# Attention and eight routed experts on one core: the gate weights of a block brought to the working buffer by two DMA transfers

## The reference

```python
def _expert_ffn(xf, Wi_e, bi_e, Wg_e, bg_e, Wo_e, bo_e, g_e, b_e):
    h = jax.nn.gelu(xf @ Wi_e + bi_e, approximate=False) * jax.nn.sigmoid(xf @ Wg_e + bg_e)
    r = xf + (h @ Wo_e + bo_e)
    mu = jnp.mean(r, axis=-1, keepdims=True)
    var = jnp.mean(jnp.square(r - mu), axis=-1, keepdims=True)
    return (r - mu) * jax.lax.rsqrt(var + EPS) * g_e + b_e
...
probs = jax.nn.softmax(xf @ Wr + br, axis=-1)
topw, topi = jax.lax.top_k(probs, K)      # K = 2 of E = 8
topw = topw / jnp.sum(topw, axis=-1, keepdims=True)
...
out = jnp.einsum('te,eth->th', c, y)      # c holds topw at topi, zero elsewhere
```

## Time and profile before

| | before |
|---|---|
| median of 3 runs | 1213.47 us |
| profiled execution, span | 1213.3 us |
| PE busy | 1083.0 us (89%) |
| VectorE (DVE) busy | 984.6 us (81%) |
| ScalarE (ACT) busy | 803.3 us (66%) |
| GpSimd (POOL) busy | 764.5 us (63%) |
| expert stage, first up matmul | 803.26 us |

### The profile page before, as it was taken

How to read it: one execution, slowest core, us unless ns; L and a number is a source line. 1 busy time by engine, 2 the same in 40 slices (tenths; PEclk the granted TensorE clock), 3 DMA queues, 4 the chain that set the end, 5 groups by cost and what they waited for, 6 DMA issues and landing times. The chain is left out here.

```text
span 1213.3 us, 27322 instructions
## 1 busy us (share of the span) xinstructions
PE 1083.0 (89%) x8520; PEld 819.8 (68%) x8520; DVE 984.6 (81%) x2792; ACT 803.3 (66%) x1804; POOL 764.5 (63%) x1359
## 2 busy tenths in 40 slices
PE   3898999999999999999999998159999999999920
PEld 1565666666666666666666664159999999999920
DVE  4776778888888888878888874659999999999959
ACT  1565666666676676666666666458888888888810
POOL 2257476676676576576576576726777777777740
PEclk9999999999999999999999999569999999999965
DMA  5223446334434434434434421521111121111138
GB/s 146 95 84 112 142 138 198 120 100 137 135 98 126 137 99 135 135 93 132 143 99 116 137 62 34 157 74 50 54 55 54 55 59 56 54 54 57 33 131 305
DMA packets 138270, 127.36 MB, mean 105 GB/s; under 512 B 71848, under 2 KB 96432, under 8 KB 138128
## 3 DMA queue, kind: packets, MB, share of 16 engines
q1 hardware_dynamic: 127184, 103.59, 28.9%
q0 software_dynamic: 8640, 17.84, 4.5%
q10 hardware_dynamic: 2304, 4.20, 0.9%
HBM read 71.13 MB, written 54.43 MB: 103 GB/s over the span
## 5 line engine op out<-in xcount | busy, mean ns | idle before, releaser
L821 ACT ACTIVATE probs<-st 128x384 f32<-128x384 f32 (+1 forms) x768 | 390.7, 526 | 177.2 <-PE st L709 165.3
L867 DVE TENSOR_REDUCE neg_max<-sa 128x2 fp32r<-128x1024 f32 (+3 forms) x384 | 392.9, 1034 | 121.4 <-PE sa L694 120.7
L647 POOL TENSOR_SCALAR_AFFINE_SELECT probs<-probs 128x128 f32<-128x128 f32 (+1 forms) x768 | 246.5, 333 | 228.7 <-ACT probs L821 220.5
L709 PE MATMUL st<-q_stack,k_pad 128*128 128x256 f32 (+2 forms) x1024 | 336.4, 370 | 9.1 <-ACT probs L821 6.6
L689 PE MATMUL sa<-k_pad,q_stack 128*128 128x256 f32 (+2 forms) x1024 | 325.4, 361 | 17.6 <-DMA k_pad<-k_scratch 10.7
L689 PEld LDWEIGHTS sa<-k_pad,q_stack 128*128 128x128 f32 x1024 | 177.5, 190 | 108.9 <-issue 72.7
L1023 POOL DMA_INDIRECT y_scratch<-z,to_row x142 | 190.0, 1338 | 35.9 <-issue 35.9
L709 PEld LDWEIGHTS st<-q_stack,k_pad 128*128 128x128 f32 x1024 | 175.6, 190 | 45.3 <-ACT probs L821 29.0
L1057 PE MATMUL up<-xt_hi,w_cur 128*128 128x256 f32 x568 | 167.3, 294 | 0.0
L722 PE MATMUL pv<-probs,v_aug 128*32 128x512 f32 (+3 forms) x2048 | 166.0, 442 | 0.0
L1058 PE MATMUL up<-xt_lo,w_cur 128*128 128x256 f32 x568 | 161.6, 285 | 0.0
(11 more groups left out here) (161 smaller groups left out, 1435.6 us busy)
## 6 DMA issues: line engine op xcount, KB each, us to landing
q_stack<-q_scratch SPq DMA_DIRECT2D x64, 256.0 KB, 2.7
k_pad<-k_scratch SPq DMA_DIRECT2D x256, 64.0 KB, 2.4
xg<-rows_scratch SPq DMA_DIRECT2D x71, 130.0 KB, 2.1
q_scratch<-q_hi SPq DMA_DIRECT2D x16, 512.0 KB, 3.1
k_scratch<-k_hi SPq DMA_DIRECT2D x16, 512.0 KB, 2.9
y<-y_scratch SPq DMA_DIRECT2D x16, 512.0 KB, 5.6
q_scratch<-q_lo SPq DMA_DIRECT2D x17, 256.0 KB, 3.2
k_scratch<-k_lo SPq DMA_DIRECT2D x17, 256.0 KB, 3.1
```

The costliest lines, as they stand in the source:

```text
L647: pool.affine_select(out=blk, in_=blk, compare_op=ALU.is_ge, fill=0.0, base=0, pattern=[[0, w], [1, P]], channel_multiplier=-1).then_inc(m ...
L709: last = nc.tensor.matmul(st[:, t % 2, at:at + w], k_pad[:, G * g + j, kk * P:(kk + 1) * P], q_stack[:, g, S - w:S], start=True, stop=True)
L821: nc.scalar.activation(probs[:, n % 2, j, lo:lo + w], st[:, k % 2, at:at + w], ACT.Exp).then_inc(exp_done, 1)
L867: V.tensor_reduce(neg_max[:, n % 2, heads[0]:heads[-1] + 1, i], scores[:, :, 0:(i + 1) * P], AX.X, ALU.max, negate=True).then_inc(sa_read, 1)
```

## The change

VectorE's `copy_weights` becomes `copy_biases`, which copies only the biases and signals a semaphore of its own, `b_copied`; ScalarE waits for it before the activations. Planes 2 and 3 of `w_cur` are now written by two DMA transfers for each block, 128 partitions x 2 KB each (256 KB), SBUF to SBUF, issued by SyncE. A transfer for block s waits until the up projections of block s-2 are done (`up_written`), and signals one of two semaphores for even and odd blocks. SyncE's own order is written anew: the rows of blocks 0 to 5, the gate weights of block 0, and then for each s the gate weights of block s+1 and the rows of block s+6. There are still eight `xg` buffers, and `rows` keeps its wait.

```diff
-        wi_copied, wg_copied = sem("wi_copied"), sem("wg_copied")
+        wi_copied, b_copied = sem("wi_copied"), sem("b_copied")
+        wg_copied = [sem(f"wg_copied{u}") for u in range(2)]
...
             regs = [sp.alloc_register(f"sp_row{u}") for u in range(UNROLL)]
-            for s in range(BLOCKS):
+            gate_regs = [sp.alloc_register(f"sp_expert{u}") for u in range(UNROLL)]
+
+            def gate_weights(s):
+                u = s % UNROLL
+                sp.reg_load(gate_regs[u], expert[0:1, s:s + 1])
+                e = sp.snap(gate_regs[u], min_val=0, max_val=E - 1)
+                if s >= 2:
+                    sp.wait_ge(up_written, 4 * s - 4)
+                for half, plane in enumerate((w_hi[1], w_lo[1])):
+                    sp.dma_start(w_cur[:, u % 2, 2 + half, :].bitcast(F32), plane[:, bass.ds(e * F, F)].bitcast(F32))\
+                        .then_inc(wg_copied[s % 2], 16)
+
+            def rows(s):
...
+            for s in range(6):
+                rows(s)
+            gate_weights(0)
+            for s in range(BLOCKS):
+                if s + 1 < BLOCKS:
+                    gate_weights(s + 1)
+                if s + 6 < BLOCKS:
+                    rows(s + 6)
+
...
-                pe.wait_ge(wg_copied, s + 1)
+                pe.wait_ge(wg_copied[s % 2], 32 * (s // 2 + 1))
...
+                act.wait_ge(b_copied, s + 1)
...
-            def copy_weights(s, u):
+            def copy_biases(s, u):
                 e = expert_of(u)
                 if not before(s, 2):
                     dve.wait_ge(up_read, 4 * s - 4)
-                V.tensor_copy(b_cur[:, u % 2, :, :], b_up[:, :, bass.ds(e * FC, FC)])
-                V.tensor_copy(w_cur[:, u % 2, 2, :], w_hi[1][:, bass.ds(e * F, F)])
-                V.tensor_copy(w_cur[:, u % 2, 3, :], w_lo[1][:, bass.ds(e * F, F)]).then_inc(wg_copied, 1)
+                V.tensor_copy(b_cur[:, u % 2, :, :], b_up[:, :, bass.ds(e * FC, FC)]).then_inc(b_copied, 1)
```

More of the change, by code:

```diff
@@ L1189, in shift @@
                 last.then_inc(z_done, 1)
-            stages(dve, [(-1, copy_weights), (3, scale), (2, mean_and_variance), (3, shift),
+            stages(dve, [(-1, copy_biases), (3, scale), (2, mean_and_variance), (3, shift),
                          (2, add_epsilon), (0, product), (-2, load_expert), (1, residual), (-2, low_x),
```

## The result

The changed kernel takes 1218.8 us (median of 4 runs, 1217.72 to 1220.99) against 1213.97 us for the kernel before on the same chip (4 runs): ratio 1.0041, 95% interval 1.0026 to 1.0055. It is slower by 4.8 us. The profiled execution took 1217.76 us with a span of 1215.9 us.

What follows compares the result with a forecast made beforehand. TensorE's matmul stream was taken to bound the expert stage. Span 1213.3 us, +4.3 start, -0.1 clock, 0 for steady state and drain gave 1217.5; with the median 0.2 above, 1217.7 us, range 1216.0 to 1220.5.

Steps and rivals of the forecast that it cites:

- The bound: Expert stage: TensorE's matmul stream sets it at 4.99 us a block; removing VectorE's copies is worth 0.
- The steady state: Expert stage: each block's transfers need 3.6 us against 6.88 us available, so they stay hidden and cost 0.
- My far end of 5.6: Steady-state transfers: slowest landing considered, 5.6 us, making the need 6.2 us with 0.7 us spare.
- Order on SyncE: SyncE's queue in the steady state: row loads and later gate weights aren't held up by the new wait.
- The start: Start of expert stage: block 0's gate weights stand behind six row loads, so TensorE's stream starts 4.3 us later.
- the holds vanish: Part of rival 2 (9 in 100), SyncE's queue at the start: 1.3 us of row-load delay may be absent, start +3.0.
- The clock: Start of expert stage: TensorE's clock rises some 5 us after the first up matmul; shift taken whole, less 0.1 us.
- The sum: Whole kernel: 1213.3 us span, +4.3 start, -0.1 clock, median 0.2 above the span, 1217.7 us, 0.35% slower.
- VectorE as the bound: Rival 1, expert stage: VectorE paces it, so 46 us come off, 1172 us; 2 in 100.
- a missed block in the steady state: Rival 4, steady state: landing over 6.3 us misses its block; at 7 us, +48 us, 1266 us; 4 in 100.
- The start under 2.4 us: Rival 2, stage start: costs under 2.4 us, not measurably slower, 1215.2 or 1215.3 us; 9 in 100.
- The crowded landing of 5.6 us at the start: Rival 3, stage start: block 0's transfers land in 5.6 us among others in flight, +7.0, 1220.4 us; 10 in 100.

Runs made afterwards that it cites:

- vector_first2: Changed kernel with VectorE copying the gate weights of blocks 0 and 1 as before, SyncE's transfers beginning with block 2: 1215.35 us, ratio 0.9997 to the kernel before.
- late4: Changed kernel with each transfer for block s waiting for all four banks of the up projections of block s-1 instead of s-2: 1333.82 us.
- late1: Changed kernel with each transfer for block s waiting for the first bank of the up projections of block s-1: 1226.51 us.
- before_again: The kernel before, unchanged, run once more for its trace: 1213.63 us in its one run.
- after_again: The changed kernel itself, unchanged, run once more: 1219.0 us (11 runs), ratio 1.0038 to the kernel before.
- gates_early: Changed kernel with SyncE issuing gate weights of blocks 0 and 1 ahead of the rows of 2 to 5: 1214.08 us, ratio 1.0002 to before.
- double: Changed kernel with each block's two planes sent once more into a spare tile that nobody reads: 1218.83 us.

## Why the prediction was right, point by point

**The bound.** Right. TensorE's stream alone sets the expert stage. VectorE went from 46.5 to 41 us busy in 50, and vector_first2 puts the value of that at 0.9997 of the time. The cost of the removed copies on the path was 0, as put, to the 1 to 2 us of its interval. My sign of VectorE near 38 us in 50 was off: I took all 0.84 us a block off its busy time. The rows of neighbouring instructions overlap in the profile (by line they add up to 313 us in 280, where VectorE is busy 261), so copies of 47 us by line took only 32 us off.

**The steady state.** Right, with the term measured: need 3.6 us by the forecast, 3.3 typical and 3.5 on average in late4, against a cover of 6.88. The parts were off in opposite directions. SyncE spends 0.62 us from the first plane's issue to the second's in the steady state (949.42 to 950.04), where I took 0.47 from the loads of rows 8, and the landing is 2.4 us in the median of late4, where I took 3.0. What the mean hid is the tail, up to 5.5 us; had the cover been 4.1, as in late1, it would have cost 7 us. My far end of 5.6, from a row of another stage, was the figure that mattered.

**Order on SyncE.** Right. Row loads still leave in time, and no transposes wait in the steady state.

**The start.** Right in mechanism and size, by terms that partly cancel. I put block 0's first plane 6.44 us after the first row load, and it left 5.32 us after it: the six row loads weren't held in this execution. The two issues are 0.72 us apart, not 0.47. The second plane landed and released TensorE 2.41 us after its issue (804.05 to 806.46), where I took 3.0 with the start. Together the first up matmul stands 8.46 us after the first row load. I had 9.9 against 5.56 for a shift of 4.3; without the hold it is 8.46 against 4.42, a shift of 4.0. The rival "the holds vanish" was half true: the one hold, 1.07 of its 1.3 us, vanished on both sides, as it belonged to one execution, so it took nothing off the difference. The other 0.3 is no hold: the sixth row load leaves 4.5 us after the first in before_again and in both traces of the changed kernel, where a pitch of 0.85 makes 4.25. Together with the clock it made the two recorded spans differ by only 2.6 us. Also, I called ScalarE's copies, ready at 803.00, the last at the old start; VectorE's ended at 803.16 and was the last. This changes nothing in the sum.

The rule that I weighed there, from the Trainium skill, DMA: Bandwidth & Descriptors (section on the anatomy of one DMA), says that most of a transfer's fixed time is the receipt of its last write and heaviest at DRAM. My estimate by it was some 0.5 us less than the rows gave (1217.7 less 0.5 is 1217.2, not 1217.3). The landing of 2.4 us in late4 is 0.3 under the 256 KB load of rows 9 and 0.6 under the 3.0 that I took, so the shorter estimate was nearer for this term. It doesn't bear the rule out: both of these transfers end in SBUF, so it is the reading side that differs, and no run here has this transfer with DRAM as its target.

**The clock.** The part I was least sure of. I took the rise as tied to the first up matmul, 5 us behind it. In the traces it came 5.3 us after it in before and 3.1 in before_again, 4.1 in after and 6.1 in after_again, and 2.5 in gates_early. So it moves the stage by some 1 us from one execution to the next of either kernel. Two traces of each don't say whether the change itself shifts it; my 0.1 us for it is neither borne out nor refuted.

**The sum.** 1217.7 against 1218.8. I set the median 0.2 us above the recorded span. The profiled run of the changed kernel shows 1.9 us between its time and its span (1217.76 and 1215.9), so the recorded execution of before, with its span of 1213.3, must have been a long one of some 1215 us (the longest of its runs took 1214.91). Its hold of 1.1 us and its late clock account for that. The forecast was saved by being made as a difference. Of the 1.1 us that are left, 0.5 is the median of before, which came out higher with its fourth run. The other 0.6 is the difference, 4.8 us against my 4.2, and it was 4.2 in the larger set of after_again: the size was met within what the runs scatter.

**The rivals.** VectorE as the bound and a missed block in the steady state are refuted by the 2414 matmuls. The start under 2.4 us didn't come. The crowded landing of 5.6 us at the start didn't either; even with double's transfers behind block 0's it came 0.7 us later only.

## What to carry to other kernels

A copy taken off an engine that isn't the bound is worth nothing, however long, and the place to look for its price is the first iteration: what used to run on an idle engine beside the loads now stands behind them in one queue. When work is moved to a queue, list that queue's first ten entries in order and ask of each what it is wanted for and when; here a few lines of order recovered all 4 us, and a first attempt that moved block 0's entry alone won some 3 of them and pushed the rest to the next block. Price a start from a difference of two points in one trace, and get a second trace of the kernel before if one row of the start looks odd.

## What the runs showed of the hardware

GpSimd's work got much faster with VectorE's copies gone, and not the scatters alone. These are groups by line from 870 to 1150 us in the changed kernel (busy us, mean ns, idle before):

```profile
L1045 POOL DMA_INDIRECT y_scratch<-z,to_row x113 | 115.5, 1022 | 28.5 <-issue 28.5
...
L1039 POOL TENSOR_TENSOR inv_dev<-inv_dev,minus_half 128x2 f32<-128x2 f32 x57 | 43.7, 767 | 95.6 <-DVE inv_dev L1191 95.6
```

Before they took 1357 and 1090 ns on average in the same stretch. I had expected 0.4 us off one of two scatters; the mean of both fell by 335 ns and the power operation by 323. The Trainium skill's page SBUF — State Buffer (section on its two separate sides) has a VectorE copy in a two-port mode, for which it names an fp32 copy from SBUF to SBUF, lock GpSimd out of a shared port pair until it ends, and this fits it. No run here took only one of the two copies away, so the mechanism is argued and not shown. A kernel that is bound by GpSimd might gain from this change what this one didn't: 55 us of 280.

The other thing not expected is the spread of a transfer of fixed size: two 256 KB planes, SBUF to SBUF, typically cost 3.3 us from the released wait to TensorE's start, and sometimes up to 5.5. The long ones all had an 8 or 16 KB packet of an instruction queue beside them, 10 of 10 in late4 and 11 of 11 in late1. Such packets come in every trace here, so a cover that is sized by the median landing alone fails in some blocks, as late1's did.
